# Moving the matrix-set loads of a retention and FFN layer from SyncE's DMA queue to ScalarE's, on 8 cores

## What is computed

```python
# x (32, 2048, 1024) f32; 16 heads of 64; FFN width 3072, int32 weights / 127
xn = layernorm(x)
q, k, v = (xn @ wq.T, xn @ wk.T, xn @ wv.T)      # split into heads
D[h, i, j] = gamma[h] ** (i - j) if i >= j else 0
y = ((q @ k.T) * D) @ v                           # per head
y = (y - mean(y)) * rsqrt(var(y) + eps)           # over time and head width, per head
attn = (y * gn_w + gn_b) @ wo.T
ffn = (silu(xn @ wg.T) * (xn @ wu.T)) @ wd.T
out = x + attn + ffn
```

## Time and profile before

| what | us |
|---|---|
| timed, median of 2 runs | 4743.76 |
| the two runs | 4735.15 and 4752.37 |
| profiled execution, its own time | 4450.39 |
| its span, slowest core | 4448.8 |
| spans of the 8 cores | 4426.1 to 4448.8 |
| TensorE busy | 3654.9 (82%) |
| VectorE busy | 1372.0 (31%) |
| ScalarE busy | 693.8 (16%) |
| GpSimd busy | 392.3 (9%) |
| SP's DMA queue (q1) | 359.22 MB, 27.6% of the 16 engines' time |
| POOL's (q0) | 167.80 MB, 15.1% |
| ACT's (q10) | 83.89 MB, 5.7% |

### The profile page before, as it was taken

How to read it: one execution, slowest core, us unless ns; L and a number is a source line. 1 busy time by engine, 2 the same in 40 slices (tenths; PEclk the granted TensorE clock), 3 DMA queues, 4 the chain that set the end, 5 groups by cost and what they waited for, 6 DMA issues and landing times.

```text
span 4448.8 us, 49430 instructions; the slowest of 8 cores (4426.1 to 4448.8 us)
## 1 busy us (share of the span) xinstructions
PE 3654.9 (82%) x17624; PEld 1643.3 (37%) x17624; DVE 1372.0 (31%) x2500; ACT 693.8 (16%) x1148; POOL 392.3 (9%) x564
## 2 busy tenths in 40 slices
PE   5306898898968889799886988889896888979898
PEld 2103333343424334343433433334343433434343
DVE  2201241424134142333324324142413414242322
ACT  1001120212002111121102212021200211111110
POOL 2320000000120000000030000000012000000003
PEclk9658989897988989798897988989798888979789
DMA  9996433342574424353465443334357343435246
GB/s 172 116 117 174 145 104 127 112 142 93 156 234 126 149 95 123 123 147 109 114 228 160 135 140 104 125 114 141 95 160 247 117 139 105 124 113 152 86 129 231
DMA packets 567184, 614.07 MB, mean 138 GB/s; under 512 B 16674, under 2 KB 438564, under 8 KB 565796
## 3 DMA queue, kind: packets, MB, share of 16 engines
q1 hardware_dynamic: 477732, 359.22, 27.6%
q0 software_dynamic: 54912, 167.80, 15.1%
q10 hardware_dynamic: 34304, 83.89, 5.7%
HBM read 560.51 MB, written 111.15 MB: 151 GB/s over the span
## 4 chain that ended last, share of the span: by engine, by line
PE 71%; DMA 12%; DVE 6%; issue 4%; ACT 3%; POOL 1%; SPq 1%; ACTq 0%; DVEq 0%; POOLq 0%
PE pb L306 70%; DMA s_acc<-sb_xb 2%; DVE sb_ha L775 2%; DVE sb_xb L1057 2%; ACT sb_yb L851 1%; DMA s_wg<-wgT 1%; DMA s_wu<-wuT 1%; DMA s_wd<-wdT 1%; DMA sb_xb<-x 1%; DVE sb_gn_acc L858 1%; SPq L937 1%; DMA out<-sb_xb 1%; DMA sb_xb<-s_acc 1%; ACT sb_ha L735 1%; POOL sb_xn L553 1%
## 5 line engine op out<-in xcount | busy, mean ns | idle before, releaser
L306 PE MATMUL pb<-sb_xn,sb_wgw 128*128 128x512 bf16 x3072 | 737.4, 383 | 207.6 <-DMA sb_wgw<-s_wg 207.6
L306 PE MATMUL pb<-sb_xn,sb_wuw 128*128 128x512 bf16 x3072 | 730.3, 381 | 0.0
L992 DVE SCALAR_TENSOR_TENSOR sb_ha<-pb,sb_silu 128x512 bf16<-128x512 f32 x384 | 265.7, 692 | 1126.2 <-PE pb L306 1096.1
L306 PE MATMUL pb<-sb_xn,sb_wset 128*128 128x512 bf16 x2048 | 479.1, 398 | 147.6 <-ACT sb_xn L468 145.1
L306 PEld LDWEIGHTS pb<-sb_xn,sb_wgw 128*128 128x128 bf16 x3072 | 301.4, 99 | 574.6 <-issue 221.0
L775 DVE TENSOR_TENSOR sb_ha<-pb,sb_mask 128x512 bf16<-128x512 f32 (+3 forms) x1024 | 418.3, 482 | 243.4 <-PE pb L306 243.3
L306 PE MATMUL pb<-sb_wdr,sb_ha 128*128 128x512 bf16 x2048 | 447.2, 379 | 0.0
L306 PEld LDWEIGHTS pb<-sb_xn,sb_wuw 128*128 128x128 bf16 x3072 | 302.0, 98 | 367.7 <-issue 9.7
L977 ACT ACTIVATE sb_silu<-pb 128x512 bf16<-128x512 f32 x384 | 228.6, 597 | 1162.0 <-PE pb L306 1161.8
L306 PE MATMUL pb<-sb_qt,sb_kt 64*128 64x512 bf16 (+3 forms) x1024 | 231.6, 422 | 214.5 <-DVE sb_ha L775 196.5
L306 PE MATMUL pb<-sb_wset,sb_xn 128*128 128x512 bf16 x1472 | 329.1, 385 | 41.7 <-POOL sb_xn L553 37.9
(11 more groups left out here) (82 smaller groups left out, 2070.8 us busy)
## 6 DMA issues: line engine op xcount, KB each, us to landing
sb_wgw<-s_wg SPq DMA_DIRECT2D x192, 512.0 KB, 4.1
sb_wuw<-s_wu SPq DMA_DIRECT2D x192, 512.0 KB, 5.5
sb_xb<-x ACTq DMA_DIRECT2D x64, 512.0 KB, 5.5
sb_wdr<-s_wd SPq DMA_DIRECT2D x64, 512.0 KB, 10.4
sb_wdr<-s_wd POOLq DMA_DIRECT2D x64, 512.0 KB, 6.7
s_acc<-sb_xb POOLq DMA_DIRECT2D x16, 2048.0 KB, 10.1
sb_xb<-s_acc ACTq DMA_DIRECT2D x16, 2048.0 KB, 13.3
out<-sb_xb POOLq DMA_DIRECT2D x64, 512.0 KB, 6.7
```

The source lines that it names most:

```text
L306: e.matmul(o, l, r, start=s1, stop=s2),
L992: e.scalar_tensor_tensor(sb["ha"][:, 512 * fm:512 * (fm + 1)], b[:], INV127, sb["silu2"][:, 512 * (fm % 2): 512 * (fm % 2 + 1)], ALU.mult, ...
```

## The change

The load of a matrix set is issued by ScalarE and takes its semaphore from group X, and no longer by SyncE from group W. Waits, source and destination are the same. There are 49 such loads in the program of a core.

```diff
     def load_wset(slot, snm, free_tok):
         src = dram[snm][:, :].rearrange("(kc p) n -> p kc n", p=128)
         dst = wset[slot][:].rearrange("p (kc n) -> p kc n", kc=8)
-        t = E.dma("sync", "W", lambda e, o=dst, i=src:
+        t = E.dma("scalar", "X", lambda e, o=dst, i=src:
                   e.dma_start(out=o, in_=i),
                   waits=[stage_done[snm], free_tok])
```

## The result

| what | before | after |
|---|---|---|
| median of all timed runs, us | 4459.30 (10 runs) | 4498.98 (11 runs) |
| ratio | 1 | 1.0093, 95% interval 1.0081 to 1.0105 |
| span of the profiled execution, us | 4448.8 | 4497.0 |
| bytes on SP's queue / ACT's, MB | 359.22 / 83.89 | 256.45 / 186.66 |

The change makes the kernel 0.9% slower, inside the 2% that were called "within 2%" but clear of no change. The forecast ratio was 1.0097, which is close. The forecast time was 4790 us in a range of 4722 to 4855 us, and the measured 4498.98 us lies outside that range. In some executions of either kernel the cores of a die run at a lower granted clock (0.75 to 0.81 instead of 0.86, in the changed kernel's at 4725.12, 4855.62 and 4997.04 us), so the ratios leave these out, and by their length the two times given for the kernel before (4735.15 and 4752.37) belong to them.

What follows compares the result with a forecast made beforehand. TensorE was taken to run nearly back to back except for a 207.6 us start stall and 11 xn-eviction waits (145.1 us). Terms 5 + 18 + 9 + 4 + 7 = +43, ratio 1.0097, on 4743.76 gave 4790 us, range 4722 to 4855.

Steps and rivals of the forecast that it cites:

- A: Program start: ACT stands at staged set loads, holding V evictions, but the 64.7 us stall tail vanishes; +5 us (0 to +15).
- B: Starts of sub-blocks 1 and 2, 8 places: earlier w_down tiles slow the s_acc write 2.3 us each; +18 us (0 to 28).
- C: Pass B, 3 of 4: windows and tiles now run beside the s_acc write, 3 us each; +9 us (0 to 15).
- D: Three sequence boundaries: the s_wk load now runs beside the output writes; +4 us (-21 to +12).
- E: Between last V and first K eviction: ACT's issue of the third set load adds 0.45 us, 15 times; +7 us (0 to 24).
- R1: Rival, no contention: added bytes fill gaps in the s_acc write, B and C cost 0; +16 us, 4761 us; chance 0.18.
- R2: Rival, SP's freedom pays: nothing competes with output writes at the boundary, D is -21; -17 us, 4726 us; chance 0.08.
- R3: Rival: ACT's ring holds the third set load while the second is in flight; +95 us, 4845 us and up; chance 0.08.
- R4: Rival: the start costs its full 62 us because window 2 stays late; total +98 us, 4848 us; chance 0.08.

Runs made afterwards that it cites:

- e4: The change, with windows 0 and 1 and SP's w_down tiles waiting for the last V matmul in all sub-blocks but the first; ratio 0.9958 to the kernel before.
- e1: The change, but SP still waits at each place where it stood before, without issuing the set load; ratio 0.9993 to the kernel before.
- e10: Kernel before with x loads behind xn evictions, windows and tiles late, plus the change; ratio 0.9674 to the kernel before, against 0.9680 without the change.
- tiles-alone run: Kernel before, set loads still on SP, its two w_down tiles issued ahead of them in each sub-block except the program's first; ratio 1.0066.
- e11: Kernel before with x loads behind evictions, windows and tiles late, and the first sub-block's set loads and first four tiles behind its last window; ratio 0.9618.

## Why the prediction was right or wrong

| term | forecast, us | slowest core | mean of 8 cores |
|---|---|---|---|
| A, start | +5 | +2.6 | |
| B, sub-block starts, 8 | +18 | +25.2 | +23.6 |
| C, pass B | +9 | +18.7, and +2.8 in the last | +13.4, and 0 in the last |
| D, boundaries, 3 | +4 | +2.4 | |
| E, ACT's issue time | +7 | +0.8, an estimate: 15 x 0.05 | |
| sum | +43 | about +53; spans +48.2 | spans +38.4 |

What makes the terms of the slowest cores 4.5 us more than the difference of their spans stays open.

**The time.** The step that failed is the last one, carrying the sum over to 4743.76 as a ratio. The 6.6% between that median and the profiled execution were not part of the kernel; the sum on the profile's own time, 4450.39 + 43 = 4493, is 6 us from the measured 4498.98. I had seen the gap and explained it away ("transfers and stalls that should stretch with the rest"), where it should have widened the range or moved the base. The direction was right, and the main mechanism: bytes beside the s_acc write. That the ratio came out at 1.0097 against 1.0093 is partly luck: on the slowest cores B and C were 17 us too low, and A, D and E 10 us too high.

**A** was right in its steps: stall from 95.35 to 307.57 (forecast 97 and 307), window 2 at 371.92 (374.0 in the forecast's sum, 367.12 before). The sub-block ends 2.6 us later: without the wait TensorE would have begun the next Q at 499.60 - 14.05 = 485.55, now at 505.50 - 17.40 = 488.10. The staging of s_wk moved from 302.45 to 306.35, 3.9 of the 5 us.

**B** had the right mechanism and too low a price: 3.15 us per 1.05 MB, where I took the middle of 1.1 and 3.4. The lower price was misread. It took the pass B write of 8.7 us for one with nothing beside it, but three output writes start 1.9 us before it lands, at 1227.0:

```profile
1225.12 1.67 POOL L1141 DMA_DIRECT2D out<-sb_xb  x3
```

With no windows or tiles beside it the write takes 7.0 to 8.8 us at the sub-block starts (e4), so the windows alone cost about 3 us there, near the upper price. The page "DMA: Bandwidth & Descriptors" of the Trainium skill, section "Issuing engines are not separate DMA queues", says that transfers of different issuers run on the same 16 DMA engines and interleave. The trace agrees: 4.3 MB went at 319 GB/s while the write was in flight. The xn waits, forecast at 16.3 us, are 17.4 to 18.5.

**C** was mis-sized most, 6.2 us per place on the slowest cores and 4.5 on average, and not 3. The write lands after 14.4 us, not the 11.5 forecast. Its price was taken near B's lower one, 2.2 us for 1.9 MB, with the reason that part of the tiles would trail the write. One did: the first tile lands at 1239.7, the second at 1245.2, 2.4 us behind the write. But the write was no shorter for it; the upper price, 6.8 us, was nearer. A little more was also left at its start than the forecast's 1.9 MB: from the first window's issue at 1222.97 until 1228.44 190 GB/s moved 1.0 MB, not 1.2.

```profile
1222.97:1228.44 5.47, 4.66 (x22) 2.18 (x23) 5.47 (x10) 0.00 (x0) 0.00 (x1) 1.00 0.67 190
```

**D** held within its bounds. **E** failed: the 0.45 us were taken as added to the path between two evictions, but ACT issues the load while the eviction before it still executes; 0.05 us were added. The test named in the forecast ("0.4 us between the last V and the first K eviction") reads 0.54 between their starts against 0.49, so the cost was not there. This is one place of 15; that e1 and e10 show no cost of the queue speaks for the others.

**The rivals.** R1 (no contention) falls by the tiles-alone run. R2 (SP's freedom pays) falls at the boundaries, which cost 2.4 us and did not give 21 back, and by pass B. R3 falls: every one of the 49 issues of a set load on ACT took 0.37 to 0.39 us. What held SP for 46.73 us at a pair of tiles, the "ring" of that rival, no run here shows. R4 falls: window 2 begins at 371.92 without a wait, so the end of the stall's tail paid for the work behind it, as forecast.

## What to carry to other kernels

A load that waits in an in-order queue also holds back everything behind it, and that can be useful: before moving it, list what it releases and which transfer, already on the path, will run beside it. When a load is placed ahead of an engine's own evictions and waits for a write, turn the order first; here that was worth 3.5%, nearly four times what the change cost. Check the times one is given against the profile, and do not carry a sum over a gap that nothing in the profile accounts for.

## What the runs showed of the hardware that was not expected

- A DMA issued on ACT between two evictions cost next to nothing: 0.37 us of issue, but only 0.05 us more between the starts of the two evictions.
- Bytes beside a write of 2.1 MB cost it nearly their full share: 1.05 MB more lengthened it by 2.6 us on average over 8 places (3.0 at the first, where 1.05 MB at the measured 319 GB/s take 3.3 us, an estimate).
- A window load's issue on SP took up to 78.40 us beside the later staging copies (e11), and 0.36 us at 372.22 in the changed kernel, when those copies had landed.
